# First stage of a four-stage transformer block: the tokens for the query product loaded already transposed from DRAM and normalized in place by GpSimd

## The reference

```python
x = x + _L0_xattn_ref(_layernorm(x, axis=-1), ctx_1024, ctx_1024, Wq, bq, Wk, bk, Wv, bv, Wo, bo)
x = x + _L0_ffn_ref(_layernorm(x, axis=-1), ...)      # experts, one token of each group of 32 to each
x = x + _L1_xattn_ref(_layernorm(x, axis=-1), ctx_1024, ctx_1024, ...)
x = x + _L1_ffn_ref(_layernorm(x, axis=-1), ...)

def _layernorm(x, axis=-1, eps=1e-05):
    m = jnp.mean(x, axis=axis, keepdims=True)
    v = jnp.var(x, axis=axis, keepdims=True)
    return (x - m) / jnp.sqrt(v + eps)
```

## Time and profile before

| | |
|---|---|
| median of 3 runs | 2046.35 us (2043.2 to 2050.53) |
| the profiled execution's own time | 2044.19 us |
| its span | 2042.5 us |
| PE busy | 1749.6 us, 86% |
| DVE busy | 1334.3 us, 65% |
| ACT busy | 1218.8 us, 60% |
| POOL busy | 604.1 us, 30% |
| granted TensorE clock, mean | 0.937 |

### The profile page before, as it was taken

One profiled execution on the slowest core, in us unless ns is written; L12 is line 12 of the kernel. 1 busy time (PEld: TensorE's weight loads), 2 busy tenths in 40 slices (PEclk: granted clock), 3 DMA queues, 4 the chain that ended last, 5 costly groups with the idle time before them and its releaser, 6 DMA issues. The chain is left out here.

```text
span 2042.5 us, 40039 instructions
## 1 busy us (share of the span) xinstructions
PE 1749.6 (86%) x14608; PEld 1088.2 (53%) x14658; DVE 1334.3 (65%) x2641; ACT 1218.8 (60%) x2361; POOL 604.1 (30%) x1107
## 2 busy tenths in 40 slices
PE   6999999999999999999985886635689789789777
PEld 2666666666666666666652553214355455455443
DVE  2766757668577685866763564414687788788775
ACT  2676666666666666666661554412576876876765
POOL 1343124321233132332300000004455455455550
PEclk9999999999999999999987997667699999999889
DMA  7543435434356354443422659987336436334200
GB/s 236 137 130 87 148 103 153 131 97 152 101 131 173 87 167 125 114 135 96 125 71 94 200 162 374 408 296 260 116 118 209 131 117 211 129 117 159 82 26 31
DMA packets 167312, 303.19 MB, mean 148 GB/s; under 512 B 26128, under 2 KB 74320, under 8 KB 158800
## 3 DMA queue, kind: packets, MB, share of 16 engines
q1 hardware_dynamic: 126496, 214.48, 32.9%
q10 hardware_dynamic: 24240, 52.57, 7.6%
q0 software_dynamic: 16384, 33.59, 7.0%
HBM read 166.09 MB, written 67.34 MB: 114 GB/s over the span
## 5 line engine op out<-in xcount | busy, mean ns | idle before, releaser
L572 DVE TENSOR_REDUCE a_negmax<-a_score 128x1 f32<-128x512 f32 x512 | 347.1, 685 | 114.7 <-PE a_score L711 107.4
L453 ACT ACTIVATE a_prob<-a_score,a_negmax 128x512 f32<-128x512 f32 x512 | 353.7, 693 | 98.4 <-DVE a_negmax L572 98.0
L334 POOL DMA_DIRECT2D a_q_stack<-a_q_parts x512 | 251.2, 499 | 532.2 <-DVE a_q_parts L566 259.8
L711 PE MATMUL a_score<-a_k_stack,a_q_stack 128*128 128x512 f32 x512 | 358.1, 700 | 21.3 <-ACT a_prob L453 12.8
L719 PEld LDWEIGHTS a_turn<-a_ident,a_prob 128*128 128x128 f32 x2048 | 254.6, 141 | 137.3 <-issue 96.2
L719 PE MATMUL a_turn<-a_ident,a_prob 128*128 128x128 f32 x2048 | 309.9, 274 | 3.6 <-ACT a_perm L429 2.0
L342 DVE COPY a_probT<-a_turn 128x512 f32<-128x512 f32 x256 | 176.4, 689 | 201.9 <-PE a_turn L719 201.6
L342 ACT COPY a_probT<-a_turn 128x512 f32<-128x512 f32 x256 | 149.9, 586 | 251.1 <-PE a_turn L719 250.2
L711 PEld LDWEIGHTS a_score<-a_k_stack,a_q_stack 128*128 128x128 f32 x512 | 97.8, 191 | 138.3 <-issue 80.8
L2058 PE MATMUL c_ff<-c_w2T,c_hqT 128*128 128x512 bf16 x485 | 133.3, 431 | 44.3 <-ACT c_hqT L1651 42.1
L793 PE MATMUL a_work<-a_cT,a_Wk 128*128 128x512 f32 x256 | 132.4, 612 | 10.2 <-DMA a_Wk<-in_L_xattn_Wk 10.2
(11 more groups left out here) (205 smaller groups left out, 3050.0 us busy)
## 6 DMA issues: line engine op xcount, KB each, us to landing
a_k_stack<-a_k_parts SPq DMA_DIRECT2D x512, 64.0 KB, 2.7
a_q_stack<-a_q_parts POOLq DMA_DIRECT2D x512, 64.0 KB, 2.4
scratch_res<-b_chosen SPq DMA_DIRECT2D x32, 1024.0 KB, 9.7
c_res<-scratch_res SPq DMA_DIRECT2D x32, 1024.0 KB, 6.7
a_weights<-in_ffn_W ACTq DMA_DIRECT2D x16, 1024.0 KB, 4.9
c_negm<-scratch_m SPq DMA_DIRECT2D x64, 256.0 KB, 5.9
a_xs<-in_x ACTq DMA_DIRECT2D x8, 1024.0 KB, 6.0
a_x<-in_x ACTq DMA_DIRECT2D x8, 1024.0 KB, 6.0
```

The source lines that it names most:

```text
L334: eng.dma_start(stack[kind][i * DH0:(i + 1) * DH0, M % 2, g, :].bitcast(F32), parts[kind][g * DH0:(g + 1) * DH0, part, :].bitcast(F32)).th ...
L453: nc.scalar.activation(prob[:, U % 4, :], score.bank(U)[:, :], ACT.Exp, bias=negmax[:, u:u + 1], accum_out=sums[:, head_of(U), tile_of(U): ...
L572: nc.vector.tensor_reduce(negmax[:, U % UNITS:U % UNITS + 1], score.bank(U)[:, :], AX.X, ALU.max, negate=True).then_inc(max_ready, 1)
L711: nc.tensor.matmul(score.bank(U)[:, :], stack["Q"][:, M % 2, g, t * P:(t + 1) * P], stack["K"][:, M % 2, g, :], start=True, stop=True).the ...
```

## The change

The tokens also come as `x_T`, laid out transposed in DRAM, and are loaded straight into `xT` (1 MB a batch, one DMA on ACT's queue). DVE still takes the statistics and the inverse root, but not the rows. It puts means and inverse deviations into `norm_cols` (128 by 8); PE turns that once ("NM", place 23), ACT copies it out and stores it to DRAM (`scratch["norm"]`, 4 KB), and loads it back to all partitions as `norm_rows` (128 by 1024, 512 KB written) at place 26. At place 28 it loads the next `xT`, once the last Q product of the batch is in. POOL then subtracts and multiplies the whole `xT` (128 by 2048) in place, between the stack of quarter 3 and the additions to x1. For batch 0 DVE does these two operations. The products at the start stand in another order.

```diff
-    TURNS = (..., (33, "R", 1, 0), (35, "XT", 0, 1), (37, "XT", 1, 1), (39, "XT", 2, 1), (41, "XT", 3, 1), ...
+    TURNS = (..., (17, "R", 0, 0), (23, "NM", 0, 1), (33, "R", 1, 0), ...
-    FIRST_TURNS = [("XT", 0, c) for c in range(C)]
-    FIRST_PRODUCTS = [("K", 0, 0), ("V", 0, 0), ("V", 0, 1), ("Q", 0, 0), ("V", 0, 2), ("V", 0, 3), ("K", 0, 1)]
-    STATS_AT, SCALE_AT, RESULT_AT = 13, 17, 21
+    FIRST_TURNS = [("NM", 0, 0)]
+    FIRST_PRODUCTS = [("K", 0, 0)] + [("V", 0, t) for t in range(T)] + [("K", 0, 1), ("Q", 0, 0)]
+    STATS_AT, SCALE_AT, COLUMNS_AT, ROWS_AT = 13, 17, 21, 26
...
@@ POOL, after the stacks of quarters 1, 2, 3
+                    if b + 1 < B:
+                        pool.wait_ge(xT_in, (b + 2) * 16)
+                        pool.wait_ge(norm_in, (b + 2) * 16)
+                        row = lambda k: norm_rows[:, k, :].unsqueeze(1).to_broadcast([P, C, S])
+                        nc.gpsimd.tensor_tensor(xT[:, :, :], xT[:, :, :], row(0), ALU.subtract).then_inc(pool_chain, 1)
+                        pool.wait_ge(pool_chain, b + 1)
+                        nc.gpsimd.tensor_tensor(xT[:, :, :], xT[:, :, :], row(1), ALU.mult).then_inc(xT_ready, 1)
@@ ACT, start
                 act.dma_start(w["Wq"][:, :, P:D], ...).then_inc(w_in["Wq"], 16)
+                act.dma_start(xT[:, :, :], A["x_T"][0]).then_inc(xT_in, 16)
                 act.dma_start(bo[:, :], ...).then_inc(loaded, 16)
@@ ACT, the turned statistics (place 23's turn, handled at place 24)
+                    if kind == "NM":
+                        if b:
+                            act.wait_ge(norm_stored, b * 16)
+                        nc.scalar.copy(norm_turned[:, :], turn.bank(j)[0:2 * T, 0:P]).then_inc(turn.free[j % 2], 1)
+                        turn.wait_read(act, 0, j)
+                        act.dma_start(scratch["norm"][b], norm_turned[:, :]).then_inc(norm_stored, 16)
+                        return
+                def load_norm(b):
+                    act.wait_ge(norm_stored, (b + 1) * 16)
+                    if b:
+                        act.wait_ge(xT_ready, b)
+                    act.sem_inc(act_parted, 1)
+                    act.dma_start(norm_rows[:, :, :].rearrange("p k s -> p (k s)"),
+                                  scratch["norm"][b].rearrange("k p -> (k p)").partition_broadcast(P)).then_inc(norm_in, 16)
@@ ACT, in the units
+                    if u == ROWS_AT and b + 1 < B:
+                        load_norm(b + 1)
+                    if u == C * 7 and b + 1 < B:
+                        work.wait_full(act, 0, jobs["Q", b, GROUPS - 1])
+                        act.dma_start(xT[:, :, :], A["x_T"][b + 1]).then_inc(xT_in, 16)
@@ DVE, start
-                norm0.on_vector(dve, chain, xs, xn).then_inc(xn_ready, 1)
-                dve.wait_ge(xn_ready, 1)
+                for t in range(T):
+                    last = norm0.tile_stats(xs, t)
+                norm0.moments(dve, chain, last)
                 dve.sem_inc(xs_read, 1)
+                norm0.scale(chain)
+                norm_columns(0)
                 low("K", 0, 0)
+                dve.wait_ge(xT_in, 16)
+                dve.wait_ge(norm_in, 16)
+                row = lambda k: norm_rows[:, k, :].unsqueeze(1).to_broadcast([P, C, S])
+                chain.step(nc.vector.tensor_tensor(xT[:, :, :], xT[:, :, :], row(0), ALU.subtract))
+                nc.vector.tensor_tensor(xT[:, :, :], xT[:, :, :], row(1), ALU.mult).then_inc(xT_ready, 1)
@@ DVE, in the units
-                        if RESULT_AT <= u < RESULT_AT + T:
-                            last = norm0.tile_result(xs, xn, u - RESULT_AT)
+                        if u == COLUMNS_AT:
+                            norm_columns(b + 1)
@@ PE, product()
+                        if kind == "Q" and n == 0:
+                            pe.wait_ge(xT_ready, b + 1)
```

More of the change, by code:

```diff
@@ L502, in _ @@
                     product_out("V", 0, t)
-                for c in range(C):
-                    turned("XT", 0, c)
-                product_out("Q", 0, 0)
+                turned("NM", 0, 0)
+                load_norm(0)
+                for t in range(T // 2, T):
+                    product_out("V", 0, t)
                 act.wait_ge(w_in["Wq"], 16)
                 nc.scalar.mul(w["Wq"][:, :, P:D], w["Wq"][:, :, P:D], SCALE).then_inc(wq_ready, 1)
-                for t in range(T // 2, T):
-                    product_out("V", 0, t)
+                product_out("Q", 0, 0)
                 act.wait_ge(xs_read, 1)
@@ L567, in low, with norm_columns @@
                                                    parts[kind][:, 0, :].bitcast(F32), ALU.add, ALU.subtract).then_inc(work.free[j % 2], 1)
+                def norm_columns(b):
+                    if b:
+                        turn.wait_full(dve, 0, entries["NM", b - 1, 0])
+                    nc.vector.tensor_copy(norm_cols[:, 0, :], norm0.mv[:, :, 0])
+                    chain.step(nc.vector.tensor_copy(norm_cols[:, 1, :], norm0.rstd[:, :]))
+                    dve.sem_inc(norm_ready, 1)
                 def maximum(U):
@@ L754, in turn_tiles @@
                         return
-                    if kind == "XT" and n == 0:
-                        pe.wait_ge(xn_ready, b + 1)
-                    elif kind == "NT" and n == 0:
+                    if kind == "NM":
+                        turn.wait_free(pe, 0, j)
+                        pe.wait_ge(norm_ready, b + 1)
+                        nc.tensor.transpose(turn.bank(j)[0:2 * T, 0:P], norm_cols[:, :, :].rearrange("p k t -> p (k t)"),
+                                            ident[:, :]).then_inc(turn.full[j % 2], 1)
+                        return
+                    if kind == "NT" and n == 0:
                         pe.wait_ge(xn1_ready, b + 1)
@@ L775, in product @@
                     if 0 in steps:
-                        turned = {("Q", 0): "XT", ("L", 0): "NT"}.get((kind, n))
+                        turned = {("L", 0): "NT"}.get((kind, n))
                         if turned:
@@ L801, in _ @@
                     product("V", 0, t, range(C))
-                for c in range(C):
-                    turn_tiles("XT", 0, c)
-                pe.wait_ge(wq_ready, 2)
-                product("Q", 0, 0, range(C))
+                turn_tiles("NM", 0, 0)
                 for t in range(T // 2, T):
@@ L809, in _ @@
                 product("K", 0, 1, range(C))
+                pe.wait_ge(wq_ready, 2)
+                product("Q", 0, 0, range(C))
                 for U in range(AHEAD):
@@ L2118, in laid_out @@
         "gate_biases": biases.reshape(T * 32, 2),
+        "x_T": inputs["x"].reshape(B, S, C, P).transpose(0, 3, 2, 1),
         "ctx_T": ctx.reshape(B, S, C, P).transpose(0, 3, 2, 1),
```

25 lines of the change are left out of this document (12 added, 13 removed).

## The result

| | before | after |
|---|---|---|
| median, same chip | 2047.72 us (4 runs, 2043.2 to 2050.53) | 2081.76 us (4 runs, 2080.6 to 2082.42) |
| span of the profiled execution | 2042.5 us | 2079.1 us |
| mean granted clock | 0.937 | 0.927 |

The ratio is 1.0171 [1.0152, 1.019]: slower by 34 us. Slower was forecast, 2062 us; the measured time is above the range's end of 2078. The forecast stood on the 2044.19 us of the profiled execution; the median of the kernel before is 3.5 us above it here.

What follows compares the result with a forecast made beforehand. PE was taken to bound the kernel, with DVE setting the pace at the second normalization (places 36 to 42). 2044.19 + 12.3 (start) + 5.4 (units: -1.65 - 7.2 + 5.2 + 4.1 + 4.9) gave 2062 us, range 2045 to 2078.

Steps and rivals of the forecast that it cites:

- The start: Before the first score and just behind it: +10.8 us for the statistics' detour over DRAM, +1.5 for the bank, +12.3 together.
- The reason for the store's delay: At the start: the statistics' store waits in ACT's queue behind wc, landing at 30.6, and is stored at about 31.0.
- Steps 0 and 1: Behind the first score: unit 0's quarter product waits for K1's bank, 2.25 us longer, of which +1.5 was taken.
- The turns: Token turns taken from PE, less one new transpose: -1.65 us in batch 0, -1.2 in each of batches 1 to 6.
- Rival 2: Places 35 to 42: the waiting goes together with the turns; units give -17.6 us, time 2038.9; chance 0.1.
- POOL's operations: POOL's subtract and multiply on 128x2048: 4.94 us each, 10.0 us for both with the wait between.
- The lock: Second normalization: DVE's small operations wait for POOL's whole running instruction; 1.3 us in each of four batches, +5.2.
- Rival 1: The lock does not reach operations of four columns; units give -8.85 us, time 2047.6; chance 0.2.
- It is just in time, and POOL works from 620.9 to 630.9.: Turned tokens land at 620.6, quarter 3's stack is issued at 620.90, so POOL need not wait for the tokens.
- rival 3: POOL is late in every batch and stands over the second normalization, 5.5 us in six batches; time 2080.6; chance 0.2.
- Batch 3: Second normalization: the stack comes later, so POOL's work ends at 503.3 against DVE's 499.65 - 0.44: +4.1 us.
- batch 4: Second normalization: cT needed 13.4 us, tokens land at some 625, about one whole POOL operation is waited for: +4.9 us.

Runs made afterwards that it cites:

- experiment 5: Changed kernel with the start's loads of bo, bc and wc issued behind the statistics' store and the load of the rows: 2086.05 us, ratio 1.0195.
- experiment 6: Changed kernel with the old start, turned tokens loaded at place 10, earlier statistics, POOL's two operations between the stacks of quarters 2 and 3: 2037.16 us, ratio 0.9959.
- experiment 2: Changed kernel without POOL's two operations in batches 1 to 7, waits and DMAs kept, tokens left unnormalized: 2053.96 us, ratio 1.0023.
- experiment 7: Changed kernel with the loads of xs and cT moved from place 26 to 30, behind the turned tokens' load: 2061.43 us, ratio 1.007.
- experiment 4: Changed kernel with the turned tokens loaded at place 18 into the buffer of xs, whose own load moves to place 45: 2058.66 us, ratio 1.0052.
- experiment 9: Changed kernel with the loads of xs and cT at place 30 and the old start: 2043.85 us, ratio 0.9989.
- experiment 8: Changed kernel's start, with POOL's operations between the stacks of quarters 2 and 3 and the earlier token load and statistics: 2051.44 us, ratio 1.0031.

## Why the prediction was right in direction and wrong in size

**The start: right, with two terms mis-sized.** The store's landing (forecast 31.0, measured 31.06), the loads' issue (44.4, measured 44.62) and the first score (58.0, measured 58.36) came as worked out. Inside, errors cancelled. The rows landed in 3.3 us, not 3.9, and DVE needed 4.6, not 5.0. Q0 took 5.37 us, partly at the lower clock, which the prediction had only as its upper bound. The reason for the store's delay was mostly wrong (experiment 5). Steps 0 and 1 cost 3.6 instead of 1.5 us, for two reasons. In step 0 it is the bank: the quarter product stands at 62.11, 3.75 us behind the first score as the prediction had worked out (before: 1.45), but it took only 1.5 of these 2.25 us for the cost, and all of them counted (2.45). In step 1 it is the clock, a term that the sum did not have: it falls to its lower level at 49.6, within PE's idle time of 13.78 us, and stays there until 66.7, and that step loses 1.14 us. With 0.3 us of the first score this is the whole difference between the 12.3 us of the forecast and the 14.7 of the trace.

**The turns: right.** Places 35 to 42 of batch 0 gave -1.95 against -1.76; that the rest of the batch comes out at -1.7 is partly chance, since 0.83 us of it were lost again where PE waits for POOL. Once nothing is held, batches 1 to 6 gave -1.2 each against -1.2 (experiment 6; in experiment 2 batch 3 gave -0.94). Rival 2, in which the waiting goes with the turns, is out.

**POOL's operations: right within 10%.** They took 4.50 to 4.57 us, not 4.94. (The figure of the GPSIMD Engine Reference of the Trainium skill, section 3.1, 4497 ns, was the nearer one. So was its 2293 ns on VectorE, where the start shows 2.29 us.)

**The lock: the rule was right.** Operations of four columns are held to the end of POOL's instruction, and without POOL's two operations nothing in the chain is held (experiment 2). Rival 1 is out.

**The step that failed: "It is just in time, and POOL works from 620.9 to 630.9."** The landing was put behind cT's 7.9 us, plus 1.6 MB at 254 GB/s, with a margin of 0.3 us to the stack. Three things were missing. The row with the 13.4 us of batch 4 was read as an exception, but with more DMA in flight it is the rule: cT takes 12.5 us at the median now. The rows, 512 KB written, need 6.7 us under this load instead of the 3.9 of the earlier trace rows. And the rate is shared with the stacks, as these windows of the changed kernel suggest, with the columns of the windows above, while the tokens loaded in batch 1 are on their way (issued at 232.72, landed 13.8 us later):

```profile
240.00:242.00 2.00, 2.00 (x12) 1.35 (x11) 1.26 (x4) 1.11 (x4) 2.00 (x5) 1.00 1.06 270
242.00:244.00 2.00, 2.00 (x13) 1.33 (x11) 1.97 (x5) 0.62 (x2) 1.69 (x4) 1.00 1.04 208
```

The engines are full (share 1.06), and POOL's and SP's stacks have their part of the 270 GB/s. How much of the lateness each of the three makes no run tells, but experiment 7 shows that the loads ahead in the queue are needed for it: issued behind the load of the tokens instead of ahead of it, they let it land in 5.4 us, and POOL is on time. So the tokens came 2.9 to 7.4 us late in four batches of six, and POOL's operations stood over the normalization. Of the time lost in batches 1 to 6 this lateness is most: one number, and 20 us less. It was rival 3, with a chance of 0.2. Its mechanism was right, its 2080.6 only by luck within 1.2 us: it had 33 us of holds over six batches where 26.8 were measured, nearly all in five, and a start of 12.3 where 14.7 were measured; the time before on which it stood was 3.5 us below the median here, and the later stages added 4.7 in the trace. With a margin of 0.3 us in a landing that rows show to vary by 5.5 us, it should have had more than the forecast's own 0.5.

**Batch 3 and batch 4.** For batch 3 +4.1 was forecast for the hold and 3.6 measured, since its stack is late without any load's doing; it stays in experiments 4, 7 and 9 and goes only when POOL's work is moved ahead of the stack (6). For batch 4 +4.9 was forecast and 7.2 measured, because two operations were held and not one. The prediction's own figures say so: cT at 619.9 and 1.6 MB at 254 GB/s behind it are 626.1, not "some 625"; then POOL subtracts until 631.1, past L144's start at 629.66, and the sum is some 6.4 instead of 4.9. In batch 2 two were held as well, the first for only 0.3 us.

**A step that was missing: the clock.** The holds took 22.1 us from DVE, but places 35 to 42 lost 19.55 + 6 x 1.2 = 26.8 us. The other 4.7 go with the 27 us at the lower clock that follow the holds. No kernel had a long hold without a low clock, but three places tell them apart in part. In batch 0 of experiment 5 nothing was held, and 3.4 us at clock 0.50 cost 1.67 us. In batch 3 of experiments 7 and 9 the hold is the same, and 3.4 us more at clock 0.50 go with 1.36 us more, of which the batch-3 figures without a hold explain 0.24 (-0.94 in experiment 8, -1.18 in experiment 6). In batches 1 and 5 of the changed kernel, though, a stretch of 3.4 us goes with only 0.3 and 0.5 us beyond the hold, and in batch 4 one of 6.8 us with 0.3. Why it costs so little there is not shown; DVE sets the pace in that place.

Open are the 1.7 us that batch 7 gains in the changed kernel, where no turn is taken away, and the few us by which the later stages differ.

## What to carry to other kernels

A long GpSimd instruction on SBUF is not hidden because its result is needed late: it is hidden only if no chain of short VectorE operations meets it, so look at what VectorE does in its whole window, give it a place with nothing of that sort, and don't hope for smaller pieces. A landing that is worked out to be just in time has no margin for a queue that is fuller than before: take it from the slowest row of its kind, move the loads that are not urgent behind it, and see what stands behind the waiting engine. Where PE has no slack, a detour over DRAM at the start costs its full latency, and here the slower clock after the pause on top.

## What the runs showed of the hardware that I had not expected

- A load of 1 MB took 5.4 us or 14.9 us at the median, by whether two other loads of 1 MB were issued 4 us before it or behind it in the same queue (experiment 7).
- A store of 4 KB to DRAM took 6.8 us among the start's loads, 5.3 us with three of them issued behind it, and under 2 us in the batches.
- 512 KB written to all partitions from 4 KB of DRAM took 3.3 us at the start and 6.7 us in the batches.
- Splitting GpSimd's instruction in four did not shorten the sum of the holds: 22.2 us over batches 1 to 6 instead of 22.1, with five short holds in batch 1 (4.9 us) where one stood before (3.2 us).
- Idling of PE for 3.18 us in the midst of dense work was followed by 3.4 us at clock 0.50, in which two matmuls took 1.72 us instead of 1.02. Where PE had no other wait, such 3.4 us cost 1.67 us (experiment 5, batch 0).
